# One-core ViT kernel: the hand-written order lists of five engines laid out anew, no products of zeros while it drains

## The reference

```
h = patches @ W.T + b ; h = [cls_tok, h]                       # (128, 17, 192)
h = h + top_k_softmax_attention(layernorm(h))                  # 12 heads of 64; 12 of 17 scores kept, mean over heads added
h = h + bitlinear_ffn(layernorm(h))                            # 8-bit rows, ternary weights, silu(gate) * up, hidden 512
h = h + gated_linear_attention(layernorm(h))                   # 12 heads of 16, causal sums, norm by head, gate from a small net
h = h + layernorm_ffn(layernorm(h))                            # 192 -> 128 -> 192 -> 192, then a layer norm
```

## Time and profile before

| | us |
|---|---|
| median of 3 runs (lowest to highest) | 645.59 (644.97 to 650.62) |
| the profiled execution | 645.34 |
| its span, first to last instruction | 643.4 |
| PE busy | 577.2 (90%) |
| DVE busy | 455.9 (71%) |
| ACT busy | 317.7 (49%) |
| POOL busy | 305.1 (47%) |

### The profile page before, as it was taken

The page is one execution under the profiler, slowest core; times in us unless marked ns, Lnnn a source line. Parts: engine busy times, 40 slices in busy tenths (PEclk is TensorE's granted clock), DMA queues, the critical chain, the costliest instruction groups (busy, mean ns, idle before and its releaser), DMA issues. The chain is left out here.

```text
span 643.4 us, 15871 instructions
## 1 busy us (share of the span) xinstructions
PE 577.2 (90%) x5229; PEld 468.1 (73%) x5229; DVE 455.9 (71%) x2101; ACT 317.7 (49%) x849; POOL 305.1 (47%) x788
## 2 busy tenths in 40 slices
PE   7999998989998989889897979797989899988985
PEld 4677877878887877778786868786877777764542
DVE  0587686778868577768695969586868677877743
ACT  2253755628371727273746465454646373725410
POOL 1011155455553546363646465555545454656564
PEclk7999999989996989898999999899989999979999
DMA  9721000000000000000000000000000000000000
GB/s 227 180 63 45 2 23 5 21 2 28 23 9 5 24 7 23 7 21 6 21 13 14 27 0 27 0 27 0 12 0 6 0 7 1 3 2 13 7 1 13
DMA packets 11062, 14.69 MB, mean 23 GB/s; under 512 B 2160, under 2 KB 8657, under 8 KB 11017
## 3 DMA queue, kind: packets, MB, share of 16 engines
q1 hardware_dynamic: 8712, 12.44, 7.3%
q10 hardware_dynamic: 2304, 1.67, 0.9%
HBM read 12.44 MB, written 1.67 MB: 22 GB/s over the span
## 5 line engine op out<-in xcount | busy, mean ns | idle before, releaser
L521 POOL TENSOR_TENSOR spread<-moments,gain_eps 119x1 f32<-119x1 f32 x57 | 10.9, 191 | 104.1 <-DVE moments L801 104.1
L522 POOL TENSOR_TENSOR rstd<-spread,minus_half 119x1 f32<-119x1 f32 (+1 forms) x95 | 55.4, 583 | 7.5
L1729 PEld LDWEIGHTS bank_embed<-norm0T,w_qkv 128*128 128x128 f32 x456 | 55.9, 194 | 3.7 <-ACT norm0T L1328 1.0
L1729 PE MATMUL bank_embed<-norm0T,w_qkv 128*128 128x119 f32 (+1 forms) x456 | 58.0, 278 | 0.0
L565 POOL TENSOR_TENSOR feat_k<-feat_qk,consts 128x238 f32<-128x238 f32 (+1 forms) x38 | 21.9, 597 | 63.3 <-DVE feat_qk L1052 63.3
L1673 PE MATMUL bank_embed<-w_tok,patchT 128*119 128x192 f32 (+1 forms) x228 | 45.6, 354 | 0.0
L1302 ACT COPY norms2T<-bank_lin 96x476 f32<-96x476 f32 (+1 forms) x19 | 10.2, 537 | 69.7 <-PE bank_lin L1554 69.7
L522 POOL TENSOR_TENSOR rstd_h<-spread_h,minus_half 119x12 f32<-119x12 f32 x19 | 43.3, 2279 | 1.5
L1673 PEld LDWEIGHTS bank_embed<-w_tok,patchT 128*119 128x119 f32 (+1 forms) x228 | 39.5, 196 | 3.1 <-issue 1.3
L1346 ACT COPY qkT<-bank_embed 128x357 f32<-128x357 f32 (+1 forms) x76 | 32.0, 445 | 18.5 <-PE bank_embed L1738 18.5
L916 DVE TENSOR_TENSOR weightsT<-bank_lin,consts 119x476 f32<-119x476 f32 (+1 forms) x57 | 34.7, 626 | 9.1 <-PE bank_lin L1934 8.8
(11 more groups left out here) (255 smaller groups left out, 1629.7 us busy)
## 6 DMA issues: line engine op xcount, KB each, us to landing
strips<-x SPq DMA_DIRECT2D x18, 336.0 KB
out<-result ACTq DMA_DIRECT2D x18, 89.2 KB
w_qkv<-L_attn_w_qkv SPq DMA_DIRECT2D x2, 576.0 KB, 7.9
w_in_raw<-L_ffn_w_in SPq DMA_DIRECT2D x1, 768.0 KB, 12.0
w_tok_raw<-L_tok_W SPq DMA_DIRECT2D x1, 576.0 KB
w_qkv_rest<-L_attn_w_qkv SPq DMA_DIRECT2D x2, 288.0 KB, 10.0
w_o<-L_attn_w_out SPq DMA_DIRECT2D x1, 576.0 KB
w_qkv_raw<-L_attn_Wqkv SPq DMA_DIRECT2D x1, 432.0 KB
```

What stands on the lines that cost most here:

```text
L522: pool.tensor_tensor(rstd_out, spread, minus_half[0:ROWS, 0:spread.shape[1]], ALU.pow) \
L1729: pe.matmul(parts((E0, E1)[s], 3)[:, j, 0:r], w_qkv0[:, tile * 128:(tile + 1) * 128], norm0T[:, s, 0:r], start=j == 0, stop=False, skip_gr ...
```

## The change

All five engines but SP get new lists. The same steps are in them for the same groups; only their order differs, in all three parts. The products of zeros: 21 instead of 12 ahead of the first weights, 48 instead of 52 in `fill`, none in `drain`. Pieces of the diff:

```diff
             pe.wait_ge(setup_zeros, 1)
-            multiply_zeros(L1, 12)
+            multiply_zeros(L1, 21)
             pe.wait_ge(ld_const, 16)
...
@@ steady of POOL @@
-                (4, p_wave), (5, p_h3_beta), (4, p_terms), (1, p_h0), (4, p_series), (4, p_overlap), (3, p_scaled), (3, p_rms),
-                (4, p_centred_sq), (4, p_den_sq), (4, p_rstd_h), (2, p_rstd1), (3, p_rstd2), (5, p_rstd4), (0, p_rstd0), (4, p_rstd3),
+                (4, p_wave), (4, p_terms), (4, p_series), (4, p_overlap), (5, p_h3_beta), (3, p_scaled), (3, p_rms), (1, p_h0),
+                (4, p_den_sq), (4, p_centred_sq), (4, p_rstd_h), (3, p_rstd2), (5, p_rstd4), (2, p_rstd1), (0, p_rstd0), (4, p_rstd3),
...
@@ steady of PE @@
-                (4, t_params), (5, t_hid1), (4, t_lin_first), (2, t_probs1), (3, t_int_in), (5, t_out4), (2, t_probs0), (4, t_lin_rest),
-                (3, t_gate), (1, t_k_main), (3, t_up), (2, t_probs2), (1, t_k_rest), (4, t_num), (2, t_att0_0), (2, t_att0_1),
+                (4, t_params), (5, t_hid1), (4, t_lin_first), (3, t_int_in), (5, t_out4), (2, t_probs0), (3, t_up), (3, t_gate),
+                (1, t_k_main), (4, t_lin_rest), (2, t_probs2), (2, t_probs1), (1, t_k_rest), (4, t_num), (2, t_att0_0), (2, t_att0_1),
...
@@ steady of ACT @@
-                (5, a_hid1), (3, a_in_T), (2, a_wide1), (2, a_wide0), (3, a_tanh_gate), (2, a_probsT0), (4, a_tanh_over), (4, a_tanh_int),
+                (2, a_wide1), (2, a_wide0), (3, a_tanh_gate), (2, a_probsT0), (1, a_v1), (4, a_tanh_over), (4, a_tanh_int), (2, a_probsT2),
...
@@ end of drain of PE @@
-                (18, t_lin_first), (17, t_out4), (18, zero_products(A0, 1)), (18, t_lin_rest), (18, zero_products(A0, 3)), (18, t_num),
-                (18, zero_products(A0, 1)), (18, t_num_turn), (18, zero_products(A0, 12)), (18, t_att1), (18, zero_products(A0, 1)),
-                (18, t_proj1), (18, zero_products(A0, 10)), (18, t_norm3), (18, zero_products(A0, 1)), (18, t_hid1),
-                (18, zero_products(A0, 1)), (18, t_out4),
+                (18, t_lin_rest), (18, t_num), (18, t_num_turn), (18, t_att1), (18, t_proj1), (18, t_norm3), (18, t_hid1), (18, t_out4),
```

More of the change, by code:

```diff
@@ L2041, in _ @@
-                (1, t_num), (3, t_att0_0), (3, t_att0_1), (5, t_patches1), (1, t_num_turn), (3, t_proj0_0), (3, t_proj0_1),
-                (2, zero_products(A0, 1)), (2, t_int_out), (4, t_dots0), (2, t_down), (1, t_att1), (5, t_embed), (4, t_dots1),
-                (2, t_norms2), (1, t_proj1), (2, t_qk1), (5, t_norm0), (2, t_hid), (5, t_q_main), (5, t_q_rest), (5, t_v0), (1, t_norm3),
-                (2, t_params), (5, t_v1), (1, t_hid1), (2, t_lin_first), (3, t_int_in), (1, t_out4), (4, t_probs0), (3, t_up), (3, t_gate),
@@ new lines, in _ @@
+                (3, t_probs2), (3, t_probs1), (1, t_num), (3, t_att0_0), (3, t_att0_1), (1, t_num_turn), (3, t_proj0_0), (3, t_proj0_1),
+                (5, t_patches0), (5, t_patches1), (2, t_int_out), (4, t_dots0), (2, t_down), (5, t_embed), (4, t_dots1), (1, t_att1),
+                (2, t_norms2), (1, t_proj1), (2, t_qk1), (5, t_norm0), (2, t_hid), (5, t_q_main), (5, t_v0), (5, t_v1), (1, t_norm3),
+                (5, t_q_rest), (2, t_params), (1, t_hid1), (2, t_lin_first), (4, t_probs1), (4, t_probs0), (3, t_int_in), (1, t_out4),
@@ L2053, in _ @@
+                (4, t_norms2), (3, t_proj1), (4, t_qk1), (7, t_norm0), (4, t_hid), (7, t_q_main), (7, t_q_rest), (7, t_v0), (3, t_norm3),
                 (7, t_v1),
@@ L2070, in _ @@
-                (17, t_att0_0), (17, t_att0_1), (15, t_num), (18, t_k_rest), (15, t_num_turn), (17, t_proj0_0), (17, t_proj0_1),
-                (16, t_int_out), (18, zero_products(A0, 1)), (18, t_dots0), (16, t_down), (18, t_dots1), (15, t_att1),
-                (15, zero_products(E0, 2)), (15, t_proj1), (16, zero_products(E0, 2)), (16, t_norms2), (16, zero_products(A0, 3)),
-                (16, t_qk1), (15, t_norm3), (16, t_hid), (15, t_hid1), (16, t_params), (15, t_out4), (16, t_lin_first), (17, t_int_in),
@@ new lines, in _ @@
+                (15, t_down), (17, t_dots0), (18, t_embed), (14, t_att1), (17, t_dots1), (15, t_norms2), (14, t_proj1), (15, t_qk1),
+                (18, t_norm0), (18, t_v0), (14, t_norm3), (15, t_hid), (14, t_hid1), (18, t_q_main), (15, t_params), (14, t_out4),
+                (18, t_q_rest), (18, t_v1), (16, t_int_in), (15, t_lin_first), (16, t_gate), (18, t_k_main), (16, t_up), (15, t_lin_rest),
+                (18, t_k_rest), (17, t_probs0), (17, t_probs1), (15, t_num), (17, t_probs2), (15, t_num_turn), (17, t_att0_0),
@@ new lines, in _ @@
+                (17, t_att0_1), (16, t_int_out), (17, t_proj0_0), (16, t_down), (17, t_proj0_1), (18, t_dots0), (15, t_att1),
+                (18, t_dots1), (15, t_proj1), (16, t_norms2), (16, t_qk1), (16, t_hid), (15, t_norm3), (15, t_hid1), (16, t_params),
+                (15, t_out4), (16, t_lin_first), (17, t_int_in), (17, t_gate), (18, t_probs1), (17, t_up), (18, t_probs0),
+                (16, t_lin_rest), (18, t_probs2), (18, t_att0_0), (16, t_num), (18, t_att0_1), (16, t_num_turn), (18, t_proj0_0),
@@ new lines, in _ @@
+                (18, t_proj0_1), (17, t_int_out), (17, t_down), (16, t_att1), (16, t_proj1), (17, t_norms2), (17, t_qk1), (17, t_hid),
+                (16, t_norm3), (16, t_hid1), (17, t_params), (18, t_int_in), (16, t_out4), (18, t_gate), (17, t_lin_first), (18, t_up),
+                (17, t_lin_rest), (17, t_num), (17, t_num_turn), (18, t_int_out), (18, t_down), (17, t_att1), (17, t_proj1),
+                (18, t_norms2), (18, t_qk1), (18, t_hid), (17, t_norm3), (18, t_params), (18, t_lin_first), (17, t_hid1), (17, t_out4),
```

385 lines of the change are left out of this document (185 added, 200 removed).

## The result

The changed kernel takes 604.30 us (median of 4 runs, 603.87 to 608.72), beside 648.11 us for the kernel before (median of 4); the ratio is 0.934, 95% interval 0.926 to 0.941.

A forecast was written before the change was run, and what follows sets the result against it. PE was taken as the bound, through its waits for att1 and v1. From 645.34 us profiled: loop -22, fill -7, start -1.5, drain +8.3 gave 623 us, range 606 to 645.

The forecast's parts named there:

- What bounds the kernel: Loop: PE bounds it; per turn it waits 2.09 us for att1 and 1.25 us for v1, leaving 26.9 us of work.
- att1 later: Ten loop turns: down product, first scores and embedding run where PE stood still, so the 2.09 us wait for att1 goes.
- What is late next: Loop: quant_in comes about 1.5 us earlier, PE 2.1 us earlier, so a new wait of 0.6 to 0.8 us at `t_int_in`.
- The gate: Loop: chain 1.2 us shorter without h3_beta and h0; `t_num` waits about 0.9 us if v1 is first, 2.0 if scaled is.
- Fill and start: Before the loop: att1 behind the embedding saves 7 us in the fill, nine more zero products save 1.5 at the start.
- The term for the start: Ahead of the first weights: nine more products of zeros gain 1.5 us, bounds -2.5 and +0.6.
- Drain: End of the kernel: lower clock without zeros +11.9, fewer zeros -3.5, `t_qk1` +1.9, earlier turns -2; sum +8.3 us.
- the sign: Drain, expected in the new profile: low clock from about 600 us, `t_qk1` of group 18 at 3 us or more.
- The zeros that were too many: Drain: zeros mostly fill waits that end elsewhere; removing the surplus ones gains 3.5 us, bounds 0 and -6.
- the turns ahead of 560: Drain's turns before 560 us: they gain like the loop's, 2 us.
- C: Rival, whole kernel: all gaps close, turns of 26.9 to 27.3 us, 602 us in total; chance 0.12.
- B: Rival, groups 16 to 18: pauses for POOL's chains drop the clock in the drain, about +30 us; chance 0.12.

The follow-up runs named there:

- the fill alone: The kernel before with the change's fill lists and 21 products of zeros ahead of the first weights, repeated lists and drain as before: 641.9 us, ratio 0.983.
- the drain alone: The kernel before with the change's drain lists, so without 100 products of zeros, fill and repeated turns as before: 655.3 us, ratio 1.006.

## Why the prediction was right and wrong

The loop gave 36.2 us where 22 were forecast, fill and start 15.5 for 8.5, the drain took 10.8 for 8.3: 14.2 + 7.0 - 2.5 is the miss of 18.7 us. The step that failed is the price of the new waits in the loop, 0.7 us at `t_int_in` and 0.9 us at `t_num`: both are nothing.

**What bounds the kernel: right.** The two gaps in the earlier trace rows, with the low clock behind them, are the loop's whole loss. Closing both gives turns of 26.65 us.

**att1 later: right, and a little undersized.** The wait went where the step said. It took the low clock with it, as said; I had put 0.45 us a turn on that clock. In the kernel before it is 30.78 - 3.44 (its waits) - 26.65 = 0.7 us, with a fall in every second turn; with att1 back in the changed kernel, where it falls in every turn, it is 1.4 us.

**What is late next: wrong, the first part of the main error.** The step forecast 0.6 to 0.8 us at `t_int_in`. The trace of the changed kernel has none. From VectorE's and ScalarE's timelines:

```profile
442.72 0.21 DVE L974 TENSOR_SCALAR quant_in<-ainv_in,rstd 119x1 f32<-119x1 f32 x1
...
443.48 0.35 ACT L1384 ACTIVATE int_in<-big_in 119x192 bf16<-119x192 f32 x1
```

int_in is there at 443.83, PE takes it at 444.10. Counted from `t_num`, quant_in ends at 442.93 - 423.05 = 19.9 us; it was 459.57 - 437.39 = 22.2, so it moved by 2.3 us and not by the 1.5 I gave it. I had counted what left VectorE's long stretch ahead of it, but not that exp_inv and probs (0.22 and 0.37 us), which stood ahead of quant_in, now stand behind it.

**The gate: the winner right, its price wrong, the second part of the main error.** The sum took the case that v1 is first, and it is; but it put a wait of 0.9 us at `t_num` on that case. There is none. In the changed kernel, `t_params` on PE and the third mask on VectorE, around the v1 shown above:

```profile
415.25 0.32 PE L1917 MATMUL bank_lin<-w_g,hidT 128*119 128x60 f32 x2
```

```profile
421.85 0.65 DVE L916 TENSOR_TENSOR weightsT<-bank_lin,consts 119x476 f32<-119x476 f32 x1
```

Counted from the start of `t_params`, v1 ended at 467.47 - 458.80 = 8.7 us before and ends at 421.94 - 415.25 = 6.7 now, 2.0 us sooner. About half of that comes from v1's own length, 0.35 us instead of 1.41; the rest is the chain, which now has product, not overlap, as its last piece. The third mask ends at 7.25 us and PE comes at 423.05 - 415.25 = 7.8: 0.5 us to spare. The step's own figures give the same: a wait of 1.25, less 1.2 for the chain, less 1.06 for the short v1, plus 0.65 for the third mask, is -0.4 us. To reach 0.9 the copy of v ahead of the tanh would have to cost 1.3 us, and tanh_int ends 0.76 us behind overlap now and 0.58 before. That v1 is first is owed to the chain too. overlap ended 0.2 us behind the start of product before (465.45 against 465.22) and 0.25 us ahead of it after (420.73 against 420.98), so tanh_int no longer holds v1. What I had drawn from the Trainium skill in this step, that v1 would stay at 1.41 us whenever the two meet, did not hold: they meet in every turn of the loop, and v1 takes 0.35.

The two waits that did not come are the 28.5 - 27.0 = 1.5 us a turn, 14 of the 19 us by which the forecast missed.

**Fill and start: mis-sized.** Forecast -8.5 together, found -15.5 in the pair of profiled executions, but about -11 by the ratio of the fill alone. Three of the 15.5 lie ahead of the first embedding (12.2 us, before 15.2), where executions of one and the same start differ by as much: with the old start it was 11.4 to 13.6 us in seven other kernels. The term for the start, -1.5, shows nothing. What the step did not see is the turn between groups 7 and 8, which the fill's end and the loop's beginning share: 10 us less in all.

**Drain: right in mechanism, near in size partly by luck.** +8.3 forecast, +10.8 between the profiled executions, +4 between medians of the drain alone. `t_qk1` of group 18 was to cost up to 3.7 us at the lower clock. It did:

```profile
570.83 3.63 PE L1910 MATMUL bank_lin<-norms2T,w_qkv 97*128 97x34 f32 x16 [0.36 <-ACT norms2T L1302]
```

The half clock began 38 us behind the embedding of group 18 (523.1 - 484.8), where the sign named 63 (600 - 536.5), and held nearly to the end, so the stretch was larger than I took. Its price stayed small: PE is idle for 27 of these last 79 us, waiting for other engines. That the longer stretch and the lower price nearly cancel is luck. The zeros that were too many (-3.5) and the turns ahead of 560 (-2) no run prices by themselves. What PE waited for in the last 62 us of the changed kernel:

```profile
PE bank_lin L1554 <- DVE att L1092: 6.2, 2, 4.8
PE bank_ffn L1554 <- DVE norm L1111: 2.4, 1, 2.4
PE bank_ffn L1554 <- ACT int_out L1409: 2.0, 1, 2.0
```

**The rivals.** C, all gaps close, was what happened, and at 602 us it nearly had the time; I gave it 0.12. Against it I had set VectorE's stretch without a pause, which counts only the engine's load and not the order in it. B fell: its drain of +30 us would have had to be more than twice what any run shows (the end grew from 106.9 to at most 120.1 us).

## What to carry to other kernels

When a change moves a step out of a chain that feeds one side of a race between VectorE and GpSimd, work out both start times in the new order, and subtract what the winner no longer waits: here one GpSimd step of 0.55 us put back in the chain cost 5 to 7 us of 604, with two and another swap in the same list 20 (2.0 us a turn). Look at what else stands in a list that is put back: 1.2 of those 2.0 us a turn had nothing to do with the race. A pause of PE at the upper clock is to be priced with the half clock behind it, 0.7 to 1.4 us a turn here; in these kernels one pause of 2 us was worse than two short ones of the same sum. Products of zeros belong in the pauses just ahead of the place where the clock first falls, though PE is nine tenths busy there, and their effect is read from the spread of single executions, not from one profile.
